# A transformer kernel whose first four attention heads get their scores from 8-row fp32 operands instead of operands stacked through DRAM

## The reference

```
mod  = silu(cond) @ W_mod + b_mod                       # shift, scale, gate
h    = ln(x) * (1 + scale_a) + shift_a
q, k, v = split(h @ W_qkv + b_qkv)                      # 16 heads of 8
x    = x + gate_a * (softmax(q k^T / sqrt(8)) v @ W_proj + b_proj)     # 512 x 512 per head
x    = x + (softmax(ln(x) W_qc  k_c^T / sqrt(8)) v_c @ W_cproj + b_cproj)  # 77 context rows
x    = x + gate_m * mlp(ln(x) modulated)
```

## Time and profile before

| what | value |
|---|---|
| median of 3 runs | 471.3 us (470.53 to 471.47) |
| span of the profiled execution | 470.6 us |
| layer 0's first row maximum on PE | 39.4 us |
| first score matmul (step 7) | 66.07 us |
| maxima transposed in step 12 | 84.25 us |

### The profile page before, as it was taken

One profiled execution on the slowest core, in us unless ns is written; L12 is line 12 of the kernel. 1 busy time (PEld: TensorE's weight loads), 2 busy tenths in 40 slices (PEclk: granted clock), 3 DMA queues, 4 the chain that ended last, 5 costly groups with the idle time before them and its releaser, 6 DMA issues.

```text
span 470.6 us, 8977 instructions
## 1 busy us (share of the span) xinstructions
PE 372.1 (79%) x3326; PEld 219.7 (47%) x3326; DVE 303.3 (64%) x1279; ACT 204.3 (43%) x304; POOL 109.5 (23%) x128
## 2 busy tenths in 40 slices
PE   0958839999989988899888788988584566675886
PEld 0735212332333156677655457764362344454454
DVE  4377928999988056666327352234979999996332
ACT  1141016666756935566432133322452555554411
POOL 8047235000010021001014100011434544444010
PEclk9979658999999998999989595556657777776989
DMA  7237560000000000000000000000000000000000
GB/s 212 50 109 219 171 168 1 2 2 3 2 1 2 0 1 1 1 2 3 0 1 1 6 1 7 3 3 0 2 2 1 1 2 1 1 1 1 1 23 24
DMA packets 10811, 12.16 MB, mean 26 GB/s; under 512 B 2378, under 2 KB 9103, under 8 KB 10767
## 3 DMA queue, kind: packets, MB, share of 16 engines
q1 hardware_dynamic: 10469, 11.55, 8.7%
q0 software_dynamic: 256, 0.01, 0.0%
q10 hardware_dynamic: 42, 0.01, 0.0%
HBM read 8.69 MB, written 2.62 MB: 24 GB/s over the span
## 4 chain that ended last, share of the span: by engine, by line
PE 53%; DVE 28%; ACT 7%; issue 7%; DMA 3%; POOL 1%; SPq 1%; ACTq 0%; DVEq 0%
PE psum L1328 6%; PE psum L1388 5%; PE psum L1356 5%; PE psum L1341 5%; DVE mx L1103 4%; DVE left L1158 4%; DVE left L1165 3%; PE psum L1229 3%; PE psum L1487 3%; PE psum L1371 3%; DVE top L1155 3%; PE psum L1399 2%; DVE top L1162 2%; PE psum L1455 2%; PE psum L1411 2%
## 5 line engine op out<-in xcount | busy, mean ns | idle before, releaser
L1103 DVE TENSOR_REDUCE mx<-psum 128x1 f32<-128x512 f32 x128 | 80.1, 681 | 15.1 <-PE psum L1328 15.0
L717 ACT ACTIVATE big<-psum 128x1024 f32<-128x1024 f32 x64 | 62.3, 1022 | 46.0 <-PE psum L1341 45.7
L547 POOL TENSOR_TENSOR rstd<-vareps,minus_half 128x4 f32<-128x4 f32 x12 | 12.2, 1019 | 199.4 <-DVE vareps L887 199.3
L1328 PE MATMUL psum<-KS,QS 72*128 72x512 bf16 x128 | 49.2, 417 | 5.2 <-DVE mx L1103 4.0
L1388 PE MATMUL psum<-kblk,qf 128*128 128x308 f32 x128 | 48.0, 508 | 1.1 <-DVE qf L1036 0.8
L1399 PE MATMUL psum<-ident,pr 128*77 128x128 f32 x256 | 39.6, 306 | 8.9 <-POOL pr L658 8.8
L1341 PE MATMUL psum<-QS,KS 75*128 75x512 bf16 x128 | 39.4, 395 | 7.8 <-issue 7.3
L1399 PEld LDWEIGHTS psum<-ident,pr 128*77 128x77 f32 x256 | 35.7, 172 | 17.2 <-POOL pr L658 12.0
L658 POOL TENSOR_TENSOR pr<-pr,early 128x616 f32<-128x616 f32 x16 | 23.9, 1493 | 56.7 <-ACT early L827 39.5
L1356 PE MATMUL psum<-big,V 128*9 128x512 f32 x256 | 34.3, 608 | 0.5 <-ACT big L717 0.5
L1328 PEld LDWEIGHTS psum<-KS,QS 72*128 72x128 bf16 x128 | 11.7, 102 | 45.7 <-DVE mx L1103 23.7
(11 more groups left out here) (191 smaller groups left out, 677.8 us busy)
## 6 DMA issues: line engine op xcount, KB each, us to landing
QS<-scr_q SPq DMA_DIRECT2D x8, 288.0 KB
KS<-scr_k SPq DMA_DIRECT2D x8, 288.0 KB
scr_q<-qp SPq DMA_DIRECT2D x2, 384.0 KB, 5.6
scr_k<-kp SPq DMA_DIRECT2D x2, 384.0 KB, 6.2
early<-in_L_xcond_w_ada_dram SPq DMA_DIRECT2D x1, 576.0 KB, 8.6
wmlp<-in_L_xcond_W_mlp_dram SPq DMA_DIRECT2D x2, 256.0 KB, 3.4
scr_k<-kp SPq DMA_DIRECT2D x2, 256.0 KB, 6.5
wm<-in_L_xcond_w_m_dram SPq DMA_DIRECT2D x1, 512.0 KB, 7.1
```

The lines of the kernel that those rows point to most:

```text
L717: freed(act.activation(pT[:, u % 2, 1024 * half:1024 * (half + 1)], ps, ACT.Exp), "sT", 0, u, half)
L1103: freed(dve.tensor_reduce(mx[:, n % 3, NT * hh + q:NT * hh + q + 1], ps, AX_X, ALU.max), "max", t, q)
L1328: filled(pe.matmul(ps, QS[b][0:ROWS, h, q * P:(q + 1) * P], KS[b][0:ROWS, h, :], start=True, stop=True), "max", j, q)
```

## The change

- For heads 0 to 3 of batch 0, POOL spreads 32 columns of the q and of the k weights to row groups (`wrows`, head j at columns 32j to 32j+7), and PE makes `Q0` and `K0` with one fp32 matmul each (`first_rows_qk`). They lie in the part of `QS[0]` that these heads' stacks used. Their row maxima are then fp32 matmuls over 8 rows, and their scores fp32 matmuls over 9 rows (row 8 of each group is 1 in `K0` and the negated maximum in `Q0`). No scratch, no three-part cut of maxima, no constant rows for them.
- The loop starts after batch 0's q and k alone. Batch 1's transposition, projection, both v, the context's keys and values, layer 1's modulation and the gates become items between steps 0 and 6 (`EARLY`).
- `mod_columns(0)` is cut in two; only shift and scale of the first norm come early. Condition and `b_mod` get a tile of their own (`first`).
- The ten `wide_rows` matmuls and three ACT copies become ten broadcast loads from DRAM (`load_wide`), five on ACT's queue and five on POOL's.
- SP's queue has batch 0's scratch and stacks 1 to 3 right after the loads of the prologue, then the maxima of the first heads, batch 1's scratch, and each stack of batch 1 behind the maxima of an earlier group. Five layer 0 weights and wqkv1 move behind them.
- On POOL, `split_k(0)` now stands behind the spreading of weights, `ln_rstd(0, 1)`, three memsets, five load issues and the context's rstd, whose statistics DVE makes after the reductions of step 0.

The core of the diff:

```diff
+EARLY = {0: ("ln",), 1: ("qk",), 2: ("v0", "mods"), 3: ("v1",), 4: ("ctx", "gates0"), 5: ("kv", "gates1"),
+         6: ("gates2",)}
+EARLY_ROOMS = {"ln": (("W", ("lnT", 0, 1)),), "qk": (("M0", ("qkv", 0, 1, "q")), ("W", ("qkv", 0, 1, "k"))),
+               "v0": (("W", ("qkv", 0, 0, "v")),), "v1": (("W", ("qkv", 0, 1, "v")),),
+               "mods": (("M0", ("mods", 1, 0)),), "ctx": (("W", ("ctxT",)),),
+               "kv": (("W", ("kc",)), ("W", ("vc",))),
+               "gates0": (("M0", ("gates", 0)),), "gates1": (("M0", ("gates", 1)),), "gates2": (("M0", ("gates", 2)),)}
...
+MOD_PARTS = (((0, 2), (2, 6)), ((0, 9),))
...
+    use("M0", "first")
+    use("M1", "mods", 0, 0)
+    use("M0", "lnT", 0, 0)
+    use("M1", "vecs")
+    use("X0", "rows", "q")
+    use("X1", "rows", "k")
+    use("M0", "qkv", 0, 0, "q")
+    use("M1", "qkv", 0, 0, "k")
+    use("W0", "mods", 0, 1)
...
+        Q0, K0 = [QS[0][:, 2 * n:2 * n + 2, :].rearrange("p h t -> p (h t)").bitcast(F32) for n in range(2)]
...
+        def load_wide(eng, *rows):
+            for n in rows:
+                name, r = WIDE[n]
+                src = ins[name[:2] + "_xcond" + name[2:]].rearrange("(r c) -> r c", c=C)[r:r + 1, :]
+                eng.dma_start(wide[:, n, :], src.broadcast_to([P, C])).then_inc(s_wide[n // 5], 16)
...
+        def first_max_rows(sp):
+
+            wait_read(sp, "mT", 0, 0)
+            for j in range(G):
+                sp.dma_start(Q0[QUAD * j + D:QUAD * j + DV, :].rearrange("o (i t) -> o i t", t=P),
+                             mneg0[NT * j:NT * (j + 1), :]).then_inc(s_mrow0, 16)
 
         @block.sync
         def _(sp):
             load_x(sp, 0)
             load_w(sp, "wmod0", "L0_xcond_W_mod")
+            load_w(sp, "wqkv0", "L0_xcond_W_qkv")
...
+            load_w(sp, "wkv0", "L0_xcond_W_kvc")
+            load_w(sp, "wkv1", "L1_xcond_w_kv")
+            load_w(sp, "wmod1", "L1_xcond_w_ada")
+            parts_to_scratch(sp, 0)
+            stacks(sp, 0, 1, 2, 3)
+            constant_rows(sp, 0)
+            load_w(sp, "wproj", "L0_xcond_W_proj")
+            first_max_rows(sp)
+            parts_to_scratch(sp, 1)
+            for name, key in (("wqc0", "W_qc"), ("wcproj", "W_cproj"), ("wmlp1", "W_mlp1"), ("wmlp2", "W_mlp2")):
                 load_w(sp, name, "L0_xcond_" + key)
-            for name, key in (("wkv1", "w_kv"), ("wmod1", "w_ada"), ("wqkv1", "w_qkv")):
-                load_w(sp, name, "L1_xcond_" + key)
-            constant_rows(sp)
-            for b in range(B):
-                stack_traffic(sp, b)
+            stacks(sp, 1, 0)
+            constant_rows(sp, 1)
             for n, (b, g) in enumerate(groups):
-                max_rows(sp, b, G * g, G, n, n % 2, s_mrow[n % 2], 3 * (n + 1))
-                if n == 0:
-                    for name, key in (("wso", "w_so"), ("wqc1", "w_q"), ("wco", "w_co"), ("wm1", "w_m1"),
-                                      ("wm2", "w_m2")):
+                if n:
+                    max_rows(sp, b, G * g, G, n, n % 2, s_mrow[n % 2], 3 * n)
+                if 0 < n < NG:
+                    stacks(sp, 1, n)
+                if n == 1:
+                    for name, key in (("wqkv1", "w_qkv"), ("wso", "w_so"), ("wqc1", "w_q"), ("wco", "w_co"),
+                                      ("wm1", "w_m1"), ("wm2", "w_m2")):
                         load_w(sp, name, "L1_xcond_" + key)
...
+            pool.memset(wrows[:, :, :, D:QUAD], 0.0).then_inc(s_wrows, 1)
...
+            def first_rows():
+                pool.wait_ge(s_w["wqkv0"], 16)
+                for n in range(2):
+                    pool.tensor_copy(wrows[:, n, :, 0:D], W["wqkv0"][:, n * C:n * C + G * D]
+                                     .rearrange("p (j d) -> p j d", j=NQ)).then_inc(s_wrows, 1)
...
-            for b in range(B):
-                ln_rstd(0, b)
+            ln_rstd(0, 0)
+            first_rows()
+            permute_qk()
+            ln_rstd(0, 1)
+            more_consts()
+            load_wide(pool, 5, 6, 7, 8, 9)
             pool.wait_ge(s_cst, 2 * B + 1)
             pool.tensor_tensor(crstd[:, :], cve[:, :], minus_half[0:S, 0:B], ALU.pow).then_inc(s_crs, 1)
-            permute_qk()
...
+            def rows_k_out():
+
+                ps = read_room(act, "rows", "k")
+                r = VECS["L0_b_qkv"] + 1
+                ins_ = act.activation(K0[:, :], ps, ACT.Identity, bias=colsF[:, 0, r:r + 1])
+                freed(ins_, "rows", "k")
...
+            ln_stats(0, 0)
+            ps = read_room(dve, "first")
+            freed(dve.tensor_copy(cols0[:, :], ps[:, 0:NV0]), "first")
+            wait_read(dve, "first")
+            dve.wait_ge(s_ht, 1)
+            dve.scalar_tensor_tensor(out=silu2[:, :], in0=half_tanh[:, :], scalar=1.0, in1=cols0[:, 0:B],
+                                     op0=ALU.add, op1=ALU.mult).then_inc(s_sil, 1)
+            dve.wait_ge(s_sil, 1)
+            dve.tensor_scalar(silu_c[:, :], silu2[:, :], 0.5, None, ALU.mult).then_inc(s_sil, 1)
+            ln_norm(0, 0)
+            mod_out(0, 0)
             dve.wait_ge(s_vecs, 16 * sum(name[:2] != "L1" for name in VECS))
             dve.wait_ge(s_vecs1, 16 * sum(name[:2] == "L1" for name in VECS))
             dve.tensor_copy(vecs_dh[:, :].rearrange("r (d h) -> r d h", h=H),
                             vecs[:, :].rearrange("r (h d) -> r d h", d=D)).then_inc(s_dh, 1)
             dve.tensor_copy(vecsF[:, :, :, 0:D],
                             vecs[:, :].rearrange("r (c j d) -> r c j d", c=NQ, j=NQ)).then_inc(s_dh, 1)
-            for b in range(B):
-                ln_norm(0, b)
             ps = read_room(dve, "vecs")
             dve.tensor_copy(cols[:, :], ps[:, 0:NV])
             dve.tensor_copy(cols_dh[:, :], ps[:, 64:64 + NV])
             freed(dve.tensor_copy(colsF[:, :, :], ps[:, 128:128 + 64 * NQ].rearrange("p (c r) -> p c r", c=NQ)[:, :, 0:NV]),
                   "vecs")
-            dve.wait_ge(s_ht, 1)
-            dve.scalar_tensor_tensor(out=silu2[:, :], in0=half_tanh[:, :], scalar=1.0, in1=cols[:, VECS["cond"]:NV],
-                                     op0=ALU.add, op1=ALU.mult).then_inc(s_sil, 1)
-            dve.wait_ge(s_sil, 1)
-            dve.tensor_scalar(silu_c[:, :], silu2[:, :], 0.5, None, ALU.mult).then_inc(s_sil, 1)
-            mod_out(0)
+            ln_stats(0, 1)
+            ln_norm(0, 1)
+
+            def rows_q_out():
+                r = VECS["L0_b_qkv"]
+                ps = read_room(dve, "rows", "q")
+                freed(dve.tensor_scalar(Q0[:, :], ps, colsF[:, 0, r:r + 1], SCALE, ALU.add, ALU.mult), "rows", "q")
+
+            wait_read(dve, "vecs")
+            rows_q_out()
...
+                    q_out(0)
                     for t in range(STEPS):
                         n, hh = divmod(t, G)
                         if t < HEADS and hh == 0 and n >= 3:
@@ -1103,9 +1163,26 @@
                                 freed(dve.tensor_reduce(mx[:, n % 3, NT * hh + q:NT * hh + q + 1], ps, AX_X, ALU.max),
                                       "max", t, q)
                             if q == 1 and hh == 0 and 1 <= n <= B * NG:
-                                split_max(n - 1, G * NT, ("mT", 0, n - 1))
+                                if n == 1:
+                                    ps = read_room(dve, "mT", 0, 0)
+                                    freed(dve.tensor_scalar(mneg0[:, :], ps[0:G * NT, 0:P], -1.0, None, ALU.mult),
+                                          "mT", 0, 0)
+                                else:
+                                    split_max(n - 1, G * NT, ("mT", 0, n - 1))
+                        if t == 0:
+                            ctx_stats()
+                            mod_out(0, 1)
                         if t == 1:
-                            mod_out(1)
+                            q_out(1)
+                        if t == 2:
+                            ctx_norm()
+                        if t == 3:
+                            v_out(0)
+                            mod_out(1, 0)
+                        if t == 4:
+                            v_out(1)
+                        if t == 6:
+                            vc_out()
...
+            def first_rows_qk():
+                pe.wait_ge(s_wrows, 3)
+                wait_read(pe, "lnT", 0, 0)
+                for n, part in enumerate("qk"):
+                    ps = open_room(pe, "rows", part)
+                    filled(pe.matmul(ps, wrows[:, n, :, :].rearrange("p j e -> p (j e)"), hT[:, 0, :],
+                                     start=True, stop=True), "rows", part)
...
+            mod_columns(0, 0)
+            ln_T(0, 0)
+            vec_columns()
+            first_rows_qk()
+            qk(0)
+            mod_columns(0, 1)
...
+                if j < G:
+                    if j == 0 and q == 0:
+                        wait_read(pe, "rows", "q")
+                        wait_read(pe, "rows", "k")
+                    ps = open_room(pe, "max", j, q)
```

(84 more changed lines are left out.)

288 lines of the change are left out of this document (130 added, 158 removed).

## The result

The changed kernel takes 489.5 us (median of four, 483.93 to 493.56) against 471.4 us before (four, 470.53 to 473.0). Its times scatter more than those of the kernel before. The profiled execution is the fastest of the four; it took 483.93 us with a span of 482.2, against a span of 470.6 before.

What follows compares the result with a forecast made beforehand. The prediction took PE (79% busy, partly at 1.2 GHz) and the wait chain up to layer 0's step 12 as decisive. Step 12's +17 less 4.5 gave +12.6 on the 470.6 span, plus 0.7: 484 us, range 462 to 492.

Steps and rivals of the forecast that it cites:

- step 12 marker: Transposition of the maxima in step 12 of layer 0's attention loop: forecast at 101.3 us, against 84.25 before.
- Part 1: Prologue, up to the start of layer 0's attention loop: starts at 17.5 us instead of 39.4.
- Part 2: Steps 0 to 3: sixteen 8-row fp32 maxima, mostly at the low clock, plus moved work, 39.2 us; step 4 at 56.7.
- Part 3: Steps 4 to 6: bf16 maxima, context work and gates, 12 us; the 7.33 us stall is gone.
- Part 4: Steps 7 to 11: fp32 scores in row-group pairs side by side, 31.3 us at the low clock, 16.2 at the fast.
- the credit: 4.5 us taken off the +17 because dense 128-row pieces should lift the clock once or twice.
- first rival: Up to step 12, a busy PE keeps the clock at 2.4 GHz: marker at 66.8, 454 us; chance 0.13.
- second rival: Slow maxima, but the clock is up by step 8 and stays for the scores: 471 to 474 us; chance 0.15.
- Pairs that don't overlap: Row-group pairs of scores run one after the other, another 14 us: 498 us; chance 0.04.
- a late transfer: Stack 1 or the second group's maxima arrive late behind weights and stacks: 486 to 490 us; chance 0.05.

Runs made afterwards that it cites:

- e1: The changed kernel run again with no edit; 489.9 us median.
- e2: The changed kernel with the first four heads' fp32 maxima taken over all 128 rows instead of 8; 470.5 us, ratio 1.0088 to the kernel before.
- e6: The changed kernel with its 8-row maxima reading bf16 copies, scores still fp32; 472.7 us, ratio 1.0000 to the kernel before.
- e3: The changed kernel with its sixteen fp32 maxima reordered so that four neighbours lie in four row groups; 480.7 us, ratio 1.0176 to the kernel before.
- e5: The changed kernel with only both halves of a score unit issued back to back; 479.3 us, ratio 1.0139 to the kernel before.
- e4: e3 plus both halves of a score unit issued back to back; 475.2 us, ratio 0.9919 to the kernel before.
- e8: The changed kernel with the edits of e2 and e5 together; 460.1 us, ratio 0.9743 to the kernel before.
- e7: The changed kernel's new order, but the first four heads use stacked bf16 operands without row groups; 461.6 us, ratio 0.9773 to the kernel before.
- e10: e7 with batch 0's keys split ahead of POOL's broadcasts and queries taken out ahead of context statistics; 457.6 us, ratio 0.9744 to the kernel before.

## Why it came out as forecast, and which terms were off

The forecast was 484 us. The two executions behind the ratio took 483.9 and 486.9, and the median of all four is 489.5. In the profile the shift at the step 12 marker is +12.2, forecast +17 less 4.5. The mechanism is the one forecast: narrow fp32 matmuls, one after the other at the low clock, eat more than the early start and the vanished stall give. That the total comes so near is luck in part. The 4.5 us taken off for stretches at the high clock came in this profile, the fastest execution; in e1 they did not, and the marker stood at 101.44, where the sum without them has 101.3.

- **Part 1** (loop start, forecast 17.5): 17.05. The first projection started at 10.95, forecast 10.2, and the eight modulation records took 0.9 us instead of 1.8, so two errors cancel.
- **Part 2** (39.2 us): 35.9, from 17.05 to the first 72-row maximum at 52.92. Each maximum is 1.78 at 0.50 as assumed, and the wait for `mod_out(0, 1)` is 1.72, forecast 1.9. Step 2's four fell into a clock of 1.00 after `qk(1)` (3.85 instead of 7.1); the forecast had put this into the sum's 4.5 and not into the part. The other terms came to 13.8, forecast 14.3. e2 shows that the rows were one cause of the price (through the clock), e6 that fp32 was the other. The assumption that a price goes by columns whatever the rows holds at one clock: 1.78 over 8 rows at 0.50, as over 128 rows before.
- **Part 3** (12 us, forecast from 56.7): 10.8, from 52.92 to the first score at 63.74. The clock was 0.90 in 57.6 to 63.4. The stall is gone.
- **Part 4** (31.3 us at the low clock, step 12's marker at 101.3 before the credit): 32.7 from 63.74 to the marker, forecast 31.3 + 1.3. The pairs run side by side, but in 2.08 us and not the 1.78 taken, because a matmul that isn't followed by its like costs 2.07 (e3): six such pairs are 1.8 us more, and the first, at the high clock, is 0.65 less. From one V product to the next it is 7.9 us, forecast 7.2 to 7.6; step 7 (4.8 us, forecast 5.3) and step 11 (3.15, forecast 4), both in part at the high clock, gave most of this back.
- **The end.** A marker later by 12.2 gave a span longer by 11.6. That the rest of the program shifts by the same amount holds in this profile and not in all: 17.2 gave 14.0 in e1, and 9.8 gave 3.3 in e5. "The change gains when step 12 starts before 83", a marker of about 84.3, fits the profiles near it: markers of 83.43, 85.13 and 86.64 (e4, e6, e2) have spans of 469.3, 470.7 and 475.4, against 84.25 and 470.6 before.

The **first rival** had its condition right. With the maxima at the high clock (e2) step 4 comes at 41.1, forecast 39.5. Its 454 was too low, since the scores are a second narrow stage that lowers the clock: 470.5 in e2, and 460.1 with that one shortened (e8). The **second rival** (slow maxima, fast scores) is near what e4 shows by another way, 475.2 against its 471 to 474; in the changed kernel as it stands the V matmuls over 128 rows did not lift the clock, at 0.50 through 18.40 us with three V products in it. Pairs that don't overlap, and a late transfer, did not occur.

What the forecast did not price alone is **the new order**. The runs split the 12.2 us at the marker of step 12 into three: the order by itself, in e7's form and against before, is -13.2. Then e6 against e7 differs mainly in the fp32 9-row scores, and besides in where the early work stands: step 4 stands at 42.43 and 42.30, step 12 at 85.13 and 71.08, so the scores, with what they do to the clock, cost 14.1. The changed kernel against e6 differs in the fp32 maxima: 96.47 - 85.13 = 11.3. Sum: -13.2 + 14.1 + 11.3 = 12.2. Each term is a difference of single profiles; with e1's marker the last would be 16.3. So the rival of the experiments, that the order loses, has fallen: the change holds a gain of 2.3% and a loss of 5%. Row groups start the loop 15 us sooner than the stacks can, and that head start is worth nothing even in e6: DVE and PE had to do the moved work somewhere, and step 4 is reached at the same 42.4.

Open: why one execution has a higher clock than another in the same later work (e1 and e5 against the changed kernel), and how much of the scatter of 10 us is the clock's alone.

## What to carry to other kernels

Price a matmul over few rows by its type at the low clock, and ask what stands beside it: 8 rows at full busy stayed at 0.50 where 128 rows held 1.00. Dropping a round trip through memory pays only as far as no other work fills that time: step 4 comes at 42.43 us without it (e6) and at 42.30 with it, issued sooner (e7), and the direct way cost twice the gain. When an edit changes operands and order together, build the order alone as well: here it was the better kernel.

## What was unexpected of the hardware

- Three fp32 matmuls over 8 rows in three row groups take 2.08 us at the low clock (e3) and eight records over 9 rows in four groups 2.09 (e4), against 2.07 for one alone (e3). In e3 the free rooms in PSUM set how many run together: the fourth waited 0.77 us for one.
- More rows are faster: a 128-row maximum costs 0.90 us and an 8-row one 1.80, since the first keeps the clock at 1.00 (e2), though 92 of its rows hold zeros.
- Work moved ahead on one engine puts its loads beside another's transfer: five broadcasts of 64 KB, issued around the scratch write's start, stood beside it when it took 5.59 us instead of 3.20 (e10). That they caused it is inferred.
